# A graph-network block with an in-kernel sort: the second layer's bias moved to TensorE, the turn of the sorting net moved within a step, x loaded up to six items ahead

## The reference, cut to what matters

```python
# x [50000,128], src [12500], edge_attr_128 [12500,128], W0 [256,128], W2, W3 [128,128]
edge_sum = jax.ops.segment_sum(edge_attr, src, num_segments=50000)
inputs = jnp.concatenate([x, edge_sum], axis=1)
h = jax.nn.elu(inputs @ W0 + b0)
h = jax.nn.elu(h @ W2 + b2)
out = h @ W3 + b3
y = x + out
m = jnp.mean(y, axis=-1, keepdims=True); v = jnp.var(y, axis=-1, keepdims=True)
return (y - m) / jnp.sqrt(v + 1e-5)
```

## Time and profile before

| what | value |
|---|---|
| median of 3 runs | 544.12 us (541.69 to 549.88) |
| the profiled execution's own time | 546.7 us |
| its span, first to last instruction | 544.9 us |
| TensorE matmul busy | 507.9 us, 93% |
| VectorE busy | 459.7 us, 84% |
| ScalarE busy | 418.9 us, 77% |
| GpSimd busy | 371.8 us, 68% |
| mean granted TensorE clock | 0.986 of full |
| moved by transfers | 96.98 MB, mean 178 GB/s |

### The profile page before, as it was taken

How to read it: one execution, slowest core, us unless ns; L and a number is a source line. 1 busy time by engine, 2 the same in 40 slices (tenths; PEclk the granted TensorE clock), 3 DMA queues, 4 the chain that set the end, 5 groups by cost and what they waited for, 6 DMA issues and landing times.

```text
span 544.9 us, 10037 instructions
## 1 busy us (share of the span) xinstructions
PE 507.9 (93%) x2881; PEld 362.2 (66%) x2881; DVE 459.7 (84%) x1216; ACT 418.9 (77%) x1534; POOL 371.8 (68%) x311
## 2 busy tenths in 40 slices
PE   6898999879979999999999999999999999999980
PEld 4465656556656767777777777777777777777670
DVE  7999888878989988898898888887889888888781
ACT  4888778768877888778777777787877877877770
POOL 6877777778742787777887777777677443333355
PEclk9999999999999999999999999999999999999995
DMA  5678989888767997776666766454445443332122
GB/s 162 183 200 252 270 278 277 249 242 249 220 196 214 262 273 212 206 207 183 184 184 181 196 187 175 132 149 135 125 135 150 122 134 117 96 101 91 55 79 53
DMA packets 87756, 96.98 MB, mean 178 GB/s; under 512 B 26403, under 2 KB 56595, under 8 KB 87703
## 3 DMA queue, kind: packets, MB, share of 16 engines
q1 hardware_dynamic: 58375, 70.67, 41.5%
q0 software_dynamic: 28896, 25.29, 19.0%
q10 hardware_dynamic: 432, 0.39, 0.3%
HBM read 58.10 MB, written 45.04 MB: 189 GB/s over the span
## 4 chain that ended last, share of the span: by engine, by line
PE 72%; DMA 10%; DVE 7%; ACT 5%; issue 3%; POOLq 1%; POOL 1%; SPq 1%
PE z_ps L663 16%; PE z_ps L664 16%; PE l_ps L617 15%; PE l_ps L653 15%; DMA x_sb<-x_items_dram 7%; PE side_ps L579 4%; PE l_ps L628 4%; ACT sq L760 2%; PE side_ps L645 2%; DVE h L1025 1%; DMA words<-word_rows_dram 1%; DVE e L1023 1%; DMA word_rows_dram<-net 1%; DVE o_sb L1056 1%; POOLq L475 1%
## 5 line engine op out<-in xcount | busy, mean ns | idle before, releaser
L663 PE MATMUL z_ps<-center,xT 128*128 128x128 f32 (+1 forms) x986 | 190.4, 275 | 1.3 <-ACT xT L731 1.3
L664 PE MATMUL z_ps<-w3c,h 128*128 128x128 f32 (+1 forms) x986 | 190.1, 275 | 0.0
L663 PEld LDWEIGHTS z_ps<-center,xT 128*128 128x128 f32 (+1 forms) x986 | 154.8, 191 | 43.2 <-issue 38.7
L487 POOL DMA_INDIRECT out_dram<-pair_edge,target_i x100 | 120.9, 1209 | 89.6 <-issue 84.9
L760 ACT ACTIVATE sq<-z_ps 128x128 f32<-128x128 f32 (+1 forms) x493 | 129.3, 278 | 67.7 <-PE z_ps L664 67.2
L468 POOL DMA_INDIRECT pair_edge<-pairs_dram,edge_i x100 | 124.6, 1246 | 45.8 <-issue 30.2
L664 PEld LDWEIGHTS z_ps<-w3c,h 128*128 128x128 f32 (+1 forms) x986 | 149.0, 191 | 0.0
L458 POOL DMA_INDIRECT x_early<-in_x_dram,src_i x100 | 122.9, 1229 | 32.8 <-issue 29.6
L653 PE MATMUL l_ps<-h,w 128*128 128x512 f32 (+1 forms) x248 | 128.3, 599 | 1.0 <-DVE h L1025 1.0
L738 ACT ACTIVATE e<-l_ps,bias 128x512 f32<-128x512 f32 (+1 forms) x150 | 102.2, 682 | 21.3 <-PE l_ps L653 14.8
L1025 DVE SCALAR_TENSOR_TENSOR h<-l_ps,neg_bias,e 128x512 f32<-128x512 f32 (+1 forms) x150 | 111.1, 741 | 5.3
(11 more groups left out here) (144 smaller groups left out, 445.2 us busy)
## 6 DMA issues: line engine op xcount, KB each, us to landing
out_dram<-o_sb SPq DMA_DIRECT2D x98, 256.0 KB, 4.0
x_sb<-x_items_dram SPq DMA_DIRECT2D x97, 256.0 KB, 4.4
pairs_dram<-x_early SPq DMA_DIRECT2D x25, 250.0 KB
keyB<-key_rows_dram SPq DMA_DIRECT2D x25, 250.0 KB, 4.3
pairs_dram<-in_edge_attr_dram SPq DMA_DIRECT2D x24, 256.0 KB
x_early<-in_x_dram,src_i POOLq DMA_INDIRECT x100, 5.4
pair_edge<-pairs_dram,edge_i POOLq DMA_INDIRECT x100, 4.5
out_dram<-pair_edge,target_i POOLq DMA_INDIRECT x100
```

What stands on the lines that cost most here:

```text
L487: nc.gpsimd.indirect_dma_start(out=out[:, :], out_offset=bass.IndirectOffsetOnAxis(ap=target_i[0:EP, c:c + 1], axis=0), in_=pair_edge[0:EP ...
L663: T.matmul(z, xT[:, c % X, j * q:(j + 1) * q], center[:], start=True, stop=False)
L664: mm = T.matmul(z, h2[:, c % H, j * q:(j + 1) * q], w3c[:], start=False, stop=True)
```

## The change

Four edits, in the words of the code:

1. `fused2`: in steps 8 to 34 the second layer's bias is added on TensorE too. `layer2` is followed by `add_bias` with the second layer's three rows; `elu` is called in its fused form (one instruction, no L1023); ScalarE's exponential takes `minus_one` as its bias. In the first steps `split_bias` splits both biases, in steps 1 to 4; `turn_b0` turns both and `make_bias1` keeps both.
2. The turn of the net stands after the second of the four blocks of `layer3`, no longer ahead of the first. On VectorE the group that begins with it starts two parts later in an even step and three parts later in an odd one (before: one part later in either).
3. x is loaded up to six items ahead, into eight slots: `UP_TO` grows from 4 loaded items at d = 0 by one or two a step until the lead is six (from d = 9 on). A load waits for the copy of the item eight loads before.
4. The fetched rows of x go straight to `pair_edge` (`x_early` is gone); `fetch_x` no longer waits for slots, and each of the 25 groups has a semaphore of its own.

```diff
-    AHEAD = 3
+    AHEAD = 6
+    X_SLOTS = 8
+    FIRST_LOADS = 3
+    UP_TO = [min(ND, d + 1 + min(AHEAD, 3 + d // 3)) for d in range(ND)]
+    LOADS = [range(UP_TO[d - 1] if d else FIRST_LOADS, UP_TO[d]) for d in range(ND)]
...
+        def fused2(s):
+            return FUSED_FROM <= s < KEY_AT
...
             def load(d):
-                if d >= SLOTS:
-                    sp.wait_ge(xT_ready, d - SLOTS + 1)
+                if d >= X_SLOTS:
+                    sp.wait_ge(xT_ready, d - X_SLOTS + 1)
...
             def fetch_x(g):
-                k = g % SLOTS
-                at_least(pool, x_paired[k], 16 * (g // SLOTS))
                 for j in range(J):
                     nc.gpsimd.indirect_dma_start(
-                        out=x_early[0:EP, k, j, :], out_offset=None, in_=x[:, :],
+                        out=pair_edge[0:EP, J * g + j, 0:P], out_offset=None, in_=x[:, :],
...
-            def layer2(c):
+            def layer2(s, c):
...
-                T.matmul(l2_ps[c % 2][:, 0:n], w2[:], h1[:, c % H, 0:n], start=True, stop=True).then_inc(l2_ready, 1)
+                ps = l2_ps[c % 2][:, 0:n]
+                mm = T.matmul(ps, w2[:], h1[:, c % H, 0:n], start=True, stop=not fused2(s))
+                if fused2(s):
+                    add_bias(1, ps, n, l2_ready)
+                else:
+                    mm.then_inc(l2_ready, 1)
...
-            def layer3(c):
+            def layer3(c, between=None):
...
                 for j in range(blocks(c)):
+                    if j == J // 2 and between:
+                        between()
...
-                elif c - SORT_AT in TURNED:
-                    beside = [lambda: None, lambda: turn_net(TURNED.index(c - SORT_AT))]
...
-                    parts.append(lambda: exp(c - 3, l2_ps[(c - 3) % 2], l2_ready, bias2, e2, exp2_ready))
+                    parts.append(lambda: exp(c - 3, l2_ps[(c - 3) % 2], l2_ready, minus_one if fused2(c) else bias2, e2, exp2_ready))
...
+            def split_bias(layer, part):
+                if (layer, part) == (1, 0):
+                    link(V.tensor_scalar(bias_rest[:], bias2[:], 1.0, None, ALU.add))
                 link(V.tensor_copy(bias_low[:], bias_rest[:]))
...
-                        elu(False, c - 3, l2_ps[(c - 3) % 2], bias2, neg_bias2, e2, exp2_ready, min2_ready, h2, h2_ready)
+                        elu(fused2(c), c - 3, l2_ps[(c - 3) % 2], bias2, neg_bias2, e2, exp2_ready, min2_ready, h2, h2_ready)
...
-                    beside = [lambda: None] * (c - SORT_AT in TURNED) + sort_group(c - SORT_AT)
+                    beside = [lambda: None] * ((2 + spared(c)) * (c - SORT_AT in TURNED)) + sort_group(c - SORT_AT)
```

More of the change, by code:

```diff
@@ L219, in gnn_resnorm @@
         end_sumT = sb("end_sumT", [P, EC])
-        x_sb = sb("x_sb", [P, SLOTS, J * P])
+        x_sb = sb("x_sb", [P, X_SLOTS, J * P])
         xT = sb("xT", [P, X, J * P])
@@ L293, in gnn_resnorm @@
         keyB_loaded = [sem(f"keyB_loaded{k}") for k in range(SLOTS)]
-        x_fetched = [sem(f"x_fetched{k}") for k in range(SLOTS)]
-        x_paired = [sem(f"x_paired{k}") for k in range(SLOTS)]
+        x_fetched = [sem(f"x_fetched{g}") for g in range(NE)]
+        x_paired = sem("x_paired")
         attr_paired = sem("attr_paired")
@@ L298, in gnn_resnorm @@
         dense_out = sem("dense_out")
-        x_loaded = [sem(f"x_loaded{k}") for k in range(SLOTS)]
+        x_loaded = [sem(f"x_loaded{k}") for k in range(X_SLOTS)]
         stored = [sem(f"stored{k}") for k in range(SLOTS)]
@@ L407, in load_keys @@
                     .then_inc(keyB_loaded[k], 16)
-            for c in range(1, AHEAD):
-                load(c)
+            for d in range(1, FIRST_LOADS):
+                load(d)
             sp.dma_start(w0e[:], W0[P:2 * P, :]).then_inc(w0e_loaded, 16)
@@ L419, in _ @@
                     sp.dma_start(words[0:EC, :], word_rows[0:E].rearrange("(c e) -> c e", e=EP)).then_inc(words_loaded, 16)
-                if item_in(c) and is_dense(c) and ITEMS[c][1] + AHEAD < ND:
-                    load(ITEMS[c][1] + AHEAD)
+                if item_in(c) and is_dense(c):
+                    for d in LOADS[ITEMS[c][1]]:
+                        load(d)
                 if item_in(c - 7) and is_dense(c - 7):
@@ L494, in _ @@
                 fetch_x(g)
-            for k in range(SLOTS):
-                pool.wait_ge(x_paired[k], 16 * len(range(k, NE, SLOTS)))
+            pool.wait_ge(x_paired, 16 * NE)
             pool.wait_ge(attr_paired, 16 * NE)
@@ L542, in turn_b0 @@
             def turn_b0():
-                pe.wait_ge(parts_split, 1)
-                T.transpose(z_ps[2][0:3, P:2 * P], bias_parts[:], ident[:]).then_inc(setup_mm, 1)
+                pe.wait_ge(parts_split, 2)
+                for layer in range(2):
+                    mm = T.transpose(z_ps[2][0:3, (layer + 1) * P:(layer + 2) * P], bias_parts[:, layer, :], ident[:])
+                mm.then_inc(setup_mm, 1)
             def turn_net(n):
@@ L599, in end_sums, with add_bias @@
                     .then_inc(end_sum_mm, 1)
-            def add_bias(ps, n, done):
-                T.matmul(ps, bias_rows[0:3, :], ones_row[0:3, 0:n], start=False, stop=True).then_inc(done, 1)
+            def add_bias(layer, ps, n, done):
+                T.matmul(ps, bias_rows[0:3, layer, :], ones_row[0:3, 0:n], start=False, stop=True).then_inc(done, 1)
             def layer1(s, c):
@@ L607, in layer1 @@
                 if is_dense(c):
-                    pe.wait_ge(x_loaded[d % SLOTS], 16 * (d // SLOTS + 1))
-                    x_in = x_sb[:, d % SLOTS, :]
+                    pe.wait_ge(x_loaded[d % X_SLOTS], 16 * (d // X_SLOTS + 1))
+                    x_in = x_sb[:, d % X_SLOTS, :]
                 else:
```

45 lines of the change are left out of this document (24 added, 21 removed).

## The result

| | before | after |
|---|---|---|
| median of 20 runs each, same session | 544.66 us (541.69 to 549.88) | 548.89 us (546.03 to 551.42) |
| ratio of the two, 95% interval | | 1.0071 [1.0048, 1.0094] |
| the profiled execution's own time, span | 546.7, 544.9 us | 546.44, 544.6 us |
| granted TensorE clock, mean | 0.986 | 0.99 |

Within 2%, as forecast, but the change costs 0.7%, 4 us, where I had said 544.2 us, no change. The median lies inside the range. The two profiled executions hide this: they are 0.3 us apart. That is the thing to explain, since all of the sum was made against the profiled one. Executions of one kernel fall into a faster and a slower state, and every ratio here is of fast ones alone, so that it need not be the quotient of the medians beside it.

The account below looks back on a forecast made before the run. TensorE was taken as the bound, kept waiting in the sort by loads of x. First steps +1.6, sort +1.8, hand-over -3.3 gave +0.1 us, 546.8 us profiled, less 2.6 for the median: 544.2 us; range 536.5 to 551 us.

Parts of the forecast that it names:

- part 4: Hand-over behind the sort: SyncE free earlier, so the words are stored 3.3 us earlier; -3.3 us, bounds -3.5 and 0.
- Late next is nothing: Behind the hand-over: once the words come earlier, TensorE runs on without a stop, so nothing is given back.
- The 2.6 us: Whole kernel: the median of runs, 544.12 us, lies this far below the profiled execution; taken off 546.8 to give 544.2 us.
- Part 1, the second bias: Sort: 27 more bias matmuls at 0.50 us, +13.5 us of TensorE; 14.0 us off VectorE.
- Both rivals with a cheaper bias: Sort: second bias costs 0.32 us, total 539.3 us, chance 0.15; or weight loads hidden, 0.21 us, total 536.4 us, chance 0.08.
- Part 2, the first steps: Before the sort: nine more VectorE instructions 0.18 us apart delay step 7 and all after it; +1.6 us, bounds 0 and 1.8.
- 27.3: First steps: step 7 starting near 27.3 us was a sign of being right; starting as early as before, of being wrong.
- Part 3, x ahead and the turn: Sort: 8.3 us of waits for x and the restarts gone; with the added biases the sort takes 117.8 us, +1.8 us.
- transfers stay in the way: Rival, sort: earlier loads only queue longer, TensorE keeps its waits for x; 8.1 us more, 552.3 us, chance 0.14.
- Small stalls: Sort: remaining TensorE waits not for x, put at 1.0 us, bounds 0 and 4.
- the floor of 116.8: Sort: TensorE's time for its 27 steps without waits after the change, 103.3 + 13.5 us.
- The hand-over doesn't get shorter: Rival, behind the sort: the words' two transfers stand behind queued x loads; +3.3 us, 547.5 us, chance 0.13.

Follow-up runs that it names:

- the last two runs: Changed kernel with the second bias back on VectorE, 543.13 us, ratio 0.9972; the same with the one-VectorE-instruction first layer kept in odd steps up to 42, 544.78 us, ratio 1.001.
- the first two of the last four: On the quiet chip: the changed kernel with no edit, 549.47 us, ratio 1.0092; the changed kernel with even steps' biases side by side, 545.05 us, ratio 1.0005.
- the three last runs: Changed kernel with biases side by side, 545.05 us; with second bias back on VectorE, 543.13 us; that with one-VectorE-instruction first layer in odd steps up to 42, 544.78 us.

## Why the prediction was right or wrong

**The time.** The forecast's class and range held; its number didn't, by 4.7 us (548.89 against 544.2), and the difference to the kernel before was 4.2 us and not 0. Two steps of the sum failed: part 4's "Late next is nothing" (below), and the last: "The median of the runs is 544.12 us, 2.6 us below the profiled one, so 544.2 us is what I predict." That the profile of after took 546.44 us where 546.8 was predicted is partly luck: it was one of the quick executions of its kernel, 2.4 us below the median, and the next one on the quiet chip took 548.8 us.

The 2.6 us aren't an offset that every kernel carries. My reading is that they lie in waits, which differ from execution to execution and which the change takes away: it turns them into bias matmuls of a fixed price, 27 x 0.51 = 13.8 us for an execution with many waits as for one with few. That the price is paid is shown on the quiet chip: without the second bias the same kernel is 6.3 us quicker. That it replaces waits that vary is argued: there is no second profile of before on the quiet chip. The runs' spread speaks for it. In the first comparison the fastest runs of the two kernels lie 4.3 us apart, the medians 4.2 and the slowest 1.5; in the last session it is 5.2, 4.7 and 0.2 us (35 runs of before, 12 of after). The other 2.1 us, from 546.8 to 548.9, are the size of part 4's error. In that next profile step 41 is 1.6 us longer than in that of after, at a lower clock, out of 2.4 us between the two. The clock of the 20 runs of after goes with that: the 8 at a mean clock of 0.989 or more took 547.72 us at most, and the 12 below it 548.2 us or more. That it is step 41 in all of them isn't shown.

**Part 1, the second bias.** Right: 0.50 predicted, 0.51 measured, 4.53 and 4.02 us a step. Both rivals with a cheaper bias have fallen for this order of instructions. The Trainium skill ("TensorE: Matmul & The Clock Gate", "Back-to-back issue gap"), which I had set against the row, agrees once two bias matmuls are neighbours: the second adds 0.21 us, where its table has 518 cycles for 512 columns, some 216 ns. The loads ahead of "What happens when you issue a matmul" come with it. So the price is 0.21 us for the matmul and 0.3 us for the change of kind there and back. I had seen "the same kind of switch" and taken its price as given; side by side, the 14 even steps save 0.30 us each.

**Part 2, the first steps.** +1.6 us predicted. From step 3 to 7 the kernels without the second split took 15.16, 15.08 and 15.12 us on the quiet chip (before and the last two runs), those with it 16.58, 16.80 and 16.47 us (after and the first two of the last four): +1.5 us, right. In the two profiles it doesn't show, since step 3 itself started at 10.50 and 9.16 us: step 7 started at 25.74 us and not at 27.3, which I had named as a sign of being wrong. The last two runs are one code up to there and have both (10.42 and 9.34 us), so this is a difference between executions and no gain of the change. It may be part of the 2.6 us above: the profiled execution of before had the late start.

**Part 3, x ahead and the turn.** Sort +1.8 us predicted, +1.23 measured. No profile with x six items ahead has TensorE waiting for x in the sort, and "transfers stay in the way" is refuted for the change (DMA busy 0.87 of the sort, no wait). Small stalls were put at 1.0 us; there were none: 117.22 us are 0.4 over the floor of 116.8, the 0.01 more of each of 41 biases. But that loading ahead removed the waits isn't shown: both other profiles with x three items ahead, of the kernel before and of the one with both biases, have none in the sort either. They are from other chips; on the quiet one this wasn't tried. What I didn't ask is what the 8.3 us are worth without the bias: loading ahead alone brought nothing that can be measured, since the net and its turns are late next.

**Part 4, the hand-over.** -3.3 us predicted, -3.55 at step 38. That number was in part luck, for the cause given (SyncE is free once x is loaded further ahead) doesn't hold by itself: the three last runs load ahead and store the words 2.7 to 6.2 us late, and two profiles with x three items ahead store them at once. What decides when SyncE is free stays open. And "Late next is nothing: TensorE runs on without a stop" failed. VectorE in steps 38 to 41 has the ordinary work and 26 small instructions on the keys, and from 163.1 us on it runs there without a gap in either kernel. VectorE in order of time in after, the end of this chain (the first row is ELU, L964 to L985 are on the keys):

```profile
166.81 0.75 DVE L1042 SCALAR_TENSOR_TENSOR h<-l_ps,neg_bias,e 128x512 f32<-128x512 f32 x1
...
168.05 0.16 DVE L964 TENSOR_TENSOR end_dup<-end_before,keyA 100x1 f32<-100x1 f32 x1
...
171.33 0.25 DVE L985 TENSOR_TENSOR dense_need<-dense_need,all_need 1x100 int32<-1x100 int32 x1
171.51 0.47 DVE L1040 TENSOR_SCALAR e<-e,b_in 128x512 f32<-128x512 f32 x1
172.01 0.75 DVE L1042 SCALAR_TENSOR_TENSOR h<-l_ps,neg_b,e 128x512 f32<-128x512 f32 x1
172.68 0.68 DVE L1073 TENSOR_TENSOR o_sb<-z_ps,rstd 128x512 f32<-128x512 f32 x1
```

In before the same `o_sb` stands at 172.90 us: VectorE is 0.2 us earlier, whatever TensorE gained. Of the 3.55 us 1.5 were left in after (steps 38 to 41: 18.40 against 19.92 us), and none in its second profile on the quiet chip (19.93 us), where the clock fell as well. The kernel before on the second chip, with the words in time, needed 18.95 us, and the kernel with the biases side by side on the quiet chip, with the words late, 19.85: an early store is mostly given back. In all eight profiles in which TensorE turns the words without a wait and the first layer's form was left alone from step 35 on, it waits 2.9 to 3.3 us for `o_sb` at the third layer of step 41. So the rival "The hand-over doesn't get shorter" had the price nearly right (+3.3 us) and the cause wrong. That VectorE was busy for 9.69 of the 10 us from 150 to 160 us stood in the trace of before, and I didn't read it.

The account of the first profiles of the two kernels then closes: +1.4 (splits) - 1.3 (early start) + 1.2 (sort) - 1.5 (hand-over) - 0.75 (42 to 124) + 0.7 (behind the last first layer, the rest of the span) = -0.3 us.

**What beats what.** Edits 2 to 4 without the first came out 0.3% below the kernel before in both sessions (0.9968 and 0.9972), each time with 1 inside the interval. It is the best of the family, and not shown to be faster. Not tried: the two biases side by side in even steps and the second on VectorE in odd ones, where it has no neighbour of its kind; by the rows that would take 13 x 0.51 = 6.6 us more off TensorE.

## What to carry to other kernels

Before moving a term from one profiled execution to the median of runs, ask what that execution has above the median: if it is waits, and the change replaces waits by fixed work, the excess may not be there to be had. A second profile of the kernel before, on the same chip, would have told what was a wait of the kernel and what one of the execution. Work put into waits fills them once and for all; it is paid in the executions that hadn't the waits, too. And when a stall of the full engine is removed, read the busy share of the next one in the same few steps: VectorE without a gap there means that most of the gain is handed back some steps later. Small matmuls of another kind (type and size) belong side by side: an order alone was worth 4.4 us here.

## What the runs showed that I had not expected

A matmul of another kind costs by its neighbours: 0.51 us alone between float32 matmuls, 0.21 us beside one like it (from 4.53 to 4.23 us a step, 41 to 27 waits of PEld). A wait of TensorE of 3.2 us was in one execution followed by the full clock and in another by 0.81 to 0.85 of it for some microseconds, for the same kernel on an equally quiet chip, which makes 1.6 us. And the same kernel took 544.7, 549.6 and 577.3 us on three chips; in the slower two the third layer's results reached ScalarE late, for a cause that the profiles don't show and that stays open.
